# Graph attention with exponentials left unscaled: node products multiplied by inverse sums that TensorE spreads, and two kinds of splitting moved to GpSimd

## The reference

```python
h = (x @ W.T).reshape(n, heads, out_ch)
e = jax.nn.leaky_relu(a_src[src] + a_dst[dst], NEG_SLOPE)
m = jax.ops.segment_max(e, dst, num_segments=n)
ex = jnp.exp(e - m[dst])
denom = jax.ops.segment_sum(ex, dst, num_segments=n)
alpha = ex / (denom[dst] + EPS)
out = jax.ops.segment_sum(alpha[:, :, None] * h[src], dst, num_segments=n)
```

## Time and profile before

| | us |
|---|---|
| median of 3 executions | 1968.64 |
| lowest and highest | 1968.46, 1969.21 |
| profiled execution: span, first to last instruction | 1967.6 |
| loop of the first part in it, first peak to last score of tile 4 | 754 to 970 |
| busy in the whole span: PE, DVE, ACT, POOL | 1855.2, 1295.7, 934.8, 151.5 |

### The profile page before, as it was taken

How to read it: one execution, slowest core, us unless ns; L and a number is a source line. 1 busy time by engine, 2 the same in 40 slices (tenths; PEclk the granted TensorE clock), 3 DMA queues, 4 the chain that set the end, 5 groups by cost and what they waited for, 6 DMA issues and landing times.

```text
span 1967.6 us, 30950 instructions
## 1 busy us (share of the span) xinstructions
PE 1855.2 (94%) x12197; PEld 1758.9 (89%) x12198; DVE 1295.7 (66%) x2485; ACT 934.8 (48%) x1551; POOL 151.5 (8%) x127
## 2 busy tenths in 40 slices
PE   6987999999999999788799999999999999999998
PEld 5876789998889999787699999999999999999998
DVE  7997767555345656888865744456566667676886
ACT  2331222325134536878534232345555556666776
POOL 0000000004000023323100000000101001001010
PEclk9997999999999999899799999999999999999999
DMA  3110002101112112010131132154656566676795
GB/s 117 49 49 1 25 25 105 33 25 60 62 49 89 73 39 94 23 38 17 65 123 61 63 104 73 73 207 183 220 193 221 214 217 240 219 261 245 283 328 199
DMA packets 36844, 234.30 MB, mean 119 GB/s; under 512 B 5964, under 2 KB 7366, under 8 KB 14680
## 3 DMA queue, kind: packets, MB, share of 16 engines
q1 hardware_dynamic: 31366, 217.41, 30.8%
q0 software_dynamic: 2656, 8.99, 2.0%
q10 hardware_dynamic: 2674, 5.87, 0.8%
HBM read 221.91 MB, written 10.35 MB: 118 GB/s over the span
## 4 chain that ended last, share of the span: by engine, by line
PE 43%; issue 3%; DVE 3%; DMA 1%; ACT 1%; POOL 0%; ACTq 0%; POOLq 0%; DVEq 0%
PE bank L2734 8%; PE bank L341 7%; PE bank L342 7%; PE bank L343 7%; PE bank L2735 4%; PE bank L2746 3%; PE bank L2750 2%; PE bank L2738 2%; PE bank L2747 2%; PE bank L2749 1%; PE bank L2737 1%; DVE weight_lo L314 1%; PE bank L2692 0%; DMA out<-ffn_y,slot_token 0%; DMA weight_raw_fifth<-in_ffn_w 0%
## 5 line engine op out<-in xcount | busy, mean ns | idle before, releaser
L314 DVE TENSOR_TENSOR weight_lo<-weight_raw,weight_hi 128x2304 fp32r<-128x2304 f32 (+1 forms) x155 | 392.3, 2534 | 53.5 <-ACT weight_hi L304 53.2
L304 ACT ACTIVATE weight_hi<-weight_raw 128x2304 fp32r<-128x2304 f32 (+1 forms) x155 | 323.3, 2087 | 69.1 <-DMA weight_raw<-in_ffn_w 48.3
L341 PE MATMUL bank<-xT_hi,weight_hi 128*128 128x320 f32 (+1 forms) x576 | 182.8, 317 | 1.6 <-DVE xT_lo L362 1.4
L342 PE MATMUL bank<-xT_lo,weight_hi 128*128 128x320 f32 (+1 forms) x576 | 178.0, 309 | 0.0
L343 PE MATMUL bank<-xT_hi,weight_lo 128*128 128x320 f32 (+1 forms) x576 | 177.7, 309 | 0.0
L341 PE MATMUL bank<-weight_hi,xT_hi 128*128 128x384 f32 (+1 forms) x480 | 161.4, 336 | 11.2 <-DVE weight_lo L314 6.2
L3114 DVE TENSOR_TENSOR hidden_tmp<-hidden_tmp,bank 128x160 f32<-128x160 f32 (+5 forms) x192 | 65.6, 342 | 159.5 <-ACT hidden_tmp L2897 159.5
L342 PE MATMUL bank<-weight_lo,xT_hi 128*128 128x384 f32 (+1 forms) x480 | 157.3, 328 | 0.0
L343 PE MATMUL bank<-weight_hi,xT_lo 128*128 128x384 f32 (+1 forms) x480 | 157.0, 327 | 0.0
L615 PE MATMUL bank<-one_hot_dst,one_hot_src 125*128 125x313 f16 x800 | 123.5, 306 | 15.2 <-ACT packed_counts L629 7.9
L2897 ACT ACTIVATE hidden_tmp<-bank,ffn_b_by_load 128x160 f32<-128x160 f32 (+5 forms) x192 | 73.6, 404 | 119.8 <-PE bank L2738 114.2
(11 more groups left out here) (496 smaller groups left out, 5062.4 us busy)
## 6 DMA issues: line engine op xcount, KB each, us to landing
weight_raw<-in_ffn_w SPq DMA_DIRECT2D x111, 1152.0 KB, 5.1
weight_raw_fifth<-in_ffn_w SPq DMA_DIRECT2D x25, 1152.0 KB, 5.1
weight_raw<-in_shared_w SPq DMA_DIRECT2D x16, 1152.0 KB, 5.0
weight_raw<-in_mix_kv SPq DMA_DIRECT2D x8, 1152.0 KB, 5.0
weight_raw<-in_gat_w SPq DMA_DIRECT2D x8, 768.0 KB, 4.2
weight_raw<-in_mix_q SPq DMA_DIRECT2D x4, 1152.0 KB, 5.0
weight_raw<-in_mix_out SPq DMA_DIRECT2D x4, 1152.0 KB
weight_raw<-in_gnn_w SPq DMA_DIRECT2D x4, 1152.0 KB, 5.1
```

Source lines behind the costliest of these rows:

```text
L304: act.activation(upper_, whole_, ACT.Copy).then_inc(*w_hi.one())
L314: dve.tensor_tensor(lower_, whole_, upper_.bitcast(F32), ALU.subtract).then_inc(*w_lo.one())
L341: pe.matmul(dst, a[0], b[0], start=first, stop=False)
L342: pe.matmul(dst, a[0], b[1], start=False, stop=False)
```

## The change

Softmax weights are no longer formed. The exponentials go to TensorE as they are, two ticks earlier (lags 3, 4 and 5 for the transposes, the halves and the node product), and the product of a pair is multiplied afterwards by the inverse sums. These stand one to a destination node, and in the product the nodes are columns; so TensorE turns the column of sums, read 128 times over, against the identity into a bank, where each row then holds all 128 inverses (lag 4), ScalarE copies it to `inverse` (lag 5), and VectorE multiplies the node product from its bank by it (lag 6). ScalarE then rectifies from on-chip memory. VectorE adds 1e-16 (or 5e37 for a node without edges) and inverts, once for each pair. `ZS` falls from 7 buffers to 5, `LAST_LAG` from 10 to 8, the rectified values get a third slot, and the last `Y_AT` ticks of groups 2 and 3 are two earlier. The lower halves of the rectified values and the six chunks of `SPLIT` are subtracted by GpSimd, in the same loop as its terms. Renamed semaphores and lists are left out of the diff.

```diff
+def weight_lo_beside(i):
+whole_, upper_, lower_ = buffers(i)
+pool.wait_ge(w_hi.semaphore, i + 1)
+pool.wait_ge(w_lo.semaphore, i)
+pool.tensor_tensor(lower_, whole_, upper_.bitcast(F32), ALU.subtract).then_inc(*w_lo.one())
...
-ZS, XS = 7, DEPTH
+ZS, XS = 5, DEPTH
...
-zT = pair("gat_zT", [P, 2, 2, 2 * P], gat)
+zT = pair("gat_zT", [P, 3, 2, 2 * P], gat)
...
+inverse = count_f32[:, 2 * TP:2 * TP + 2 * P]
...
-LAST_LAG = 10
+LAST_LAG = 8
...
-Y_AT = {10 * grp + tick: (grp, t) for grp in range(4) for t, tick in enumerate((12, 13, 18, 19, 21) if grp < 3 else (12, 13, 16, 17, 18))}
+Y_AT = {10 * grp + tick: (grp, t) for grp in range(4) for t, tick in enumerate({2: (12, 13, 16, 17, 18), 3: (10, 11, 14, 15, 16)}.get(grp, (12, 13, 18, 19, 21)))}
...
+    return pairs_of[q][2] // 2
...
-    return (3 * grp + t0 // 2) % 2
-def sums_after(q):
-    grp, h, t0, n = pairs_of[q]
-    return y_full.at(2 * (grp * TT + t0 + n))
+    return y_full.at(2 * ((grp - 1) * TT + t0 + n))
...
-    for u in range(N1):
-        terms(u, *units[u][0:3])
+    for i in range(N1 + LAST_LAG):
+        if i < N1:
+            terms(i, *units[i][0:3])
+        if i in SPLIT:
+            weight_lo_beside(SPLIT[i])
+        q = pair_closing(i, 6)
+        if q is not None:
+            grp, h, t0, n = pairs_of[q]
+            hi, lo = at(zT, ALL, z_slot(q), h, slice(0, n * P))
+            pool.wait_ge(*z_hi.at(q + 1))
+            pool.tensor_tensor(lo, zt[:, q % 2, 0:n * P], hi.bitcast(F32), ALU.subtract).then_inc(*z_lo.one())
...
-        q = pair_closing(i, 7)
+        q = pair_closing(i, 5)
...
-            bank = ring.next(z_relu.at(q + 1))
+            bank = ring.next(z_scaled.at(q + 1))
...
-        u = unit(i, 5)
+        u = unit(i, 3)
         if u is not None:
-            turn_unit(u, e_scaled.at(u + 1))
+            turn_unit(u, e_exp.at(u + 1))
+        q = pair_closing(i, 4)
+        if q is not None:
+            grp, h, t0, n = pairs_of[q]
+            pe.wait_ge(*e_summed.at(q + 1))
+            bank = ring.next(inverse_kept.at(q + 1))
+            inverse_banks.append(bank)
+            for t in range(n):
+                end = pe.transpose(bank[:, t * P:(t + 1) * P], total[:, grp % 2, h, t0 + t:t0 + t + 1].broadcast_to([P, P]), ident[:, :])
+            end.then_inc(*inverse_full.one())
...
+        if grp > 1 and t == 0:
+            act.wait_ge(*aggregated(grp - 2))
...
-        q = pair_closing(i, 8)
-        if q is not None:
-            grp, h, t0, n = pairs_of[q]
-            act.wait_ge(*z_full.at(q + 1))
-            if q >= 2:
-                act.wait_ge(*z_lo.at(q - 1))
-            act.activation(zt[:, q % 2, 0:n * P], z_banks[q][:, 0:n * P], ACT.Relu, bias=b1[:, 2 * grp + h:2 * grp + h + 1]).then_inc(*z_relu.one())
-            act.wait_ge(*z_relu.now())
-            if q >= 4:
-                act.wait_ge(*sums_after(q - 4))
-            upper(at(zT, ALL, z_slot(q), h, slice(0, n * P)), zt[:, q % 2, 0:n * P]).then_inc(*z_hi.one())
...
-        u = unit(i, 6)
+        u = unit(i, 4)
         if u is not None:
             if u >= XS:
                 act.wait_ge(*z_full.at(units[u - XS][4] + 1))
             turned_upper(u, at(exT, ALL, u % XS, ALL, ALL))
-        u = unit(i, 4)
-        if u is not None:
-            grp, h, t = units[u][0:3]
-            e = edge_w[:, u % ZS, :]
-            act.wait_ge(*e_summed.at(u + 1))
-            act.activation(e, e, ACT.Copy, scale=total[:, grp % 2, h, t:t + 1]).then_inc(*e_scaled.one())
+        q = pair_closing(i, 5)
+        if q is not None:
+            n = pairs_of[q][3]
+            act.wait_ge(*inverse_full.at(q + 1))
+            if q:
+                act.wait_ge(*z_scaled.at(q))
+            act.activation(inverse[:, 0:n * P], inverse_banks[q][:, 0:n * P], ACT.Copy).then_inc(*inverse_kept.one())
+        q = pair_closing(i, 6)
+        if q is not None:
+            grp, h, t0, n = pairs_of[q]
+            act.wait_ge(*z_scaled.at(q + 1))
+            z = zt[:, q % 2, 0:n * P]
+            act.activation(z, z, ACT.Relu, bias=b1[:, 2 * grp + h:2 * grp + h + 1]).then_inc(*z_relu.one())
+            act.wait_ge(*z_relu.now())
+            if grp:
+                act.wait_ge(*sums_before(q))
+            upper(at(zT, ALL, z_slot(q), h, slice(0, n * P)), z).then_inc(*z_hi.one())
...
+        own_step(dve.tensor_scalar(least_sum[:, :], edge_peak[:, :], -1.0, 5.0e37, ALU.is_lt, ALU.mult))
+        own_step(dve.tensor_scalar(least_sum[:, :], least_sum[:, :], 1e-16, None, ALU.add))
...
-        q = pair_closing(i, 8)
+        q = pair_closing(i, 6)
         if q is not None:
...
-            dve.wait_ge(*z_hi.at(q + 1))
-            lower(at(zT, ALL, z_slot(q), h, slice(0, n * P)), zt[:, q % 2, 0:n * P]).then_inc(*z_lo.one())
-        u = unit(i, 6)
+            dve.wait_ge(*z_full.at(q + 1))
+            dve.wait_ge(*inverse_kept.at(q + 1))
+            if q >= 2:
+                dve.wait_ge(*z_lo.at(q - 1))
+            dve.tensor_tensor(zt[:, q % 2, 0:n * P], z_banks[q][:, 0:n * P], inverse[:, 0:n * P], ALU.mult).then_inc(*z_scaled.one())
+        u = unit(i, 4)
         if u is not None:
             turned_lower(u, at(exT, ALL, u % XS, ALL, ALL))
-        u = unit(i, 3)
-        if u is not None:
-            grp, h, t = units[u][0:3]
-            tot = total[:, grp % 2, h, t:t + 1]
-            dve.wait_ge(*e_exp.at(u + 1))
-            own_step(dve.tensor_scalar(tot, tot, 1e-16, None, ALU.add))
-            own_step(dve.reciprocal(tot, tot))
-            dve.tensor_tensor(tot, tot, has_edge[:, t:t + 1], ALU.mult).then_inc(*e_summed.one())
         u = unit(i, 1)
         if u is not None:
             peak(u, *units[u][0:3])
+        if pair_closing(i, 3) is not None:
+            grp, h, t0, n = pairs_of[pair_closing(i, 3)]
+            sums = total[:, grp % 2, h, t0:t0 + n]
+            dve.wait_ge(*e_exp.at(i - 3 + 1))
+            own_step(dve.tensor_tensor(sums, sums, least_sum[:, t0:t0 + n], ALU.add))
+            dve.reciprocal(sums, sums).then_inc(*e_summed.one())
...
-            weight_lo(SPLIT[i])
+            done["lo"] += 1
...
+            dve.wait_ge(w_lo.semaphore, c0 + 8)
```

More of the change, by code:

```diff
@@ L524, in counting_attention @@
          q_full, sums_ready, acted, q_ready, q_hi, q_lo, o_full, o_hi, o_lo, out_full, out_added, pads_blank, pads_hi, pads_lo) = sigs(
-            "one_hot_made", "one_hot_used", "counts_read", "edges_counted", "kv_full", "kv_copied", "kv_ready", "kv_hi", "kv_lo", "heads_full", "heads_kept",
+            "one_hot_made", "one_hot_used", "counts_read", "edges_counted", "kv_full", "kv_copied_or_inverse_full", "kv_ready", "kv_hi", "kv_lo", "heads_full", "heads_or_inverse_kept",
             "att_hi", "att_lo", "q_full", "q_low", "q_exp", "q_ready", "q_hi", "q_lo", "attended_full", "attended_hi", "attended_lo", "sum_full", "sum_added",
@@ L1831, in graph_attention @@
                  "att_rows_landed", "node_full", "node_hi", "node_lo", "scored", "score_turned", "score_hi", "score_lo", "rows_full", "rows_kept",
-                 "edge_acted", "edge_made", "edge_exp", "edge_summed", "edge_scaled", "ex_turned", "ex_hi", "ex_lo", "hidden_full", "hidden_acted", "hidden_hi", "hidden_lo",
+                 "edge_acted", "edge_made", "edge_exp", "edge_summed", "hidden_scaled", "kv_copied_or_inverse_full", "heads_or_inverse_kept", "ex_turned", "ex_hi", "ex_lo", "hidden_full", "hidden_acted", "hidden_hi", "hidden_lo",
                  "gat_y_full", "gat_y_added", "scored2", "h2_hi", "h2_lo", "gat_sum_full", "gat_sum_added")
@@ L1838, in graph_attention @@
          att_in, h_full, h_hi, h_lo, scored, score_turned, score_hi, score_lo, rows_full, rows_kept,
-         e_acted, e_made, e_exp, e_summed, e_scaled, ex_turned, ex_hi, ex_lo, z_full, z_relu, z_hi, z_lo,
+         e_acted, e_made, e_exp, e_summed, z_scaled, inverse_full, inverse_kept, ex_turned, ex_hi, ex_lo, z_full, z_relu, z_hi, z_lo,
          y_full, y_added, scored2, h2_hi, h2_lo, o_full, o_added) = sigs(*names)
@@ L1851, in graph_attention @@
         has_edge = sb("gat_has_edge", [P, TT], F32, gat)
+        least_sum = sb("gat_least_sum", [P, TT], F32, gat)
         scores = sb("gat_scores", [P, 2, TT, 4], F32, gat)
@@ L1892, in graph_attention @@
         h_banks, turn_banks, row_banks, ex_banks, z_banks, y_banks, o_banks = [], [], [], [], [], [], []
+        inverse_banks = []
         units, pairs_of = [], []
@@ L1944, in z_slot, with sums_before @@
         def z_slot(q):
+            return pairs_of[q][2] // 2
+        def sums_before(q):
             grp, h, t0, n = pairs_of[q]
-            return (3 * grp + t0 // 2) % 2
-        def sums_after(q):
-            grp, h, t0, n = pairs_of[q]
-            return y_full.at(2 * (grp * TT + t0 + n))
+            return y_full.at(2 * ((grp - 1) * TT + t0 + n))
         def w1_chunk(grp):
```

## The result

The changed kernel takes 1985.66 us (median of 4 executions, 1982.65 to 1987.15); the kernel before, beside it on the same chip, 1968.93 (1968.46 to 1972.5). The ratio is 1.0075, 95% interval 1.0054 to 1.0096: slower, where 1955.1 was forecast, and outside the range.

A forecast was written before the change was run, and what follows sets the result against it. ScalarE was taken to bound group 3, TensorE at a reduced clock ticks 15 to 19 and 25 to 29, no engine ticks 10 to 14 and 20 to 24. Terms -3 + 2 - 7.5 - 4 - 1 = -13.5 gave median 1955.1, range 1949 to 1963.

The forecast's parts named there:

- transposes come two ticks earlier: -1: Fill, 43.3 us with TensorE busy 38.93 on the stage before: earlier transposes save 1 us, bounds 0 and -3.
- a bank comes back a tick later as before: Ring of eight banks, one more bank per pair: costs nothing, at worst inside the bounds.
- Ticks 15 to 19 and 25 to 29: Stretches preparing the next group: 24.1 us each, 7.5 us less in all, bounds -12.4 and -2.
- the sum from five starts: TensorE's work in ticks 15 to 19 and 25 to 29, priced from five traced starts: 22.1 us at full clock.
- gain not there: Rival: TensorE's ticks stay but for moved products (-2), group 3 gains half; -3.5 us, median 1965; chance 13%.
- Ticks 10 to 14 and 20 to 24: Stretches where GpSimd takes over five weight chunks: 2 us more for both, bounds -3 and +8.
- Group 3: Up to its last peak, 35.90 us: ScalarE needs 5.2 less, of which 3 us is gained, bounds 0 and -5.2.
- Drain: After the last peak, 32.0 us: two ticks fewer save 4 us of idle, bounds 0 and -5.
- The shared read decides: Rival: GpSimd never lets VectorE in between instructions, each chunk costing the peak 5.3 us; +5.5, median 1974; chance 9%.
- The multiplication, which reads a bank: On VectorE: not held up by GpSimd, costs 0.44 us and replaces a lower half of 0.59.
- the 3.76 taken in proportion: GpSimd's price for a 1536-column weight chunk: 3.76 us, scaled from 1.567 for 640 columns, an upper end.
- the 0.63 in proportion: GpSimd's price for a pair's lower half of 256 columns: 0.63 us, scaled from its 640-column term.

The follow-up runs named there:

- e5: Changed kernel with VectorE's multiplication by the inverses moved ahead of the same tick's preparations; 1975.26 us, ratio 1.0027 to the kernel before.
- e2: Changed kernel with the old lags (transposes 5, halves 6, product 7, multiplication 8); 1973.88 us, ratio 1.0025 to the kernel before.
- e6: Changed kernel with the old lags and the multiplication ahead of the same tick's preparations; 1964.95 us, ratio 0.9963 to the kernel before.
- e7: As e6, with the weight chunks' lower halves back on VectorE; 1960.93 us, ratio 0.9949 to the kernel before.
- e10: As e5 (short lags, early multiplication), with the weight chunks' lower halves back on VectorE; 1971.69 us, ratio 1.0005 to the kernel before.
- e1: Changed kernel with the halves of units 0 and 1 made at the end of tick 5; 1983.57 us, ratio 1.0067 to the kernel before.
- e11: As e10, with the halves of units 0 and 1 made at the end of tick 5; 1965.38 us, ratio 0.9984 to the kernel before.
- e9: As e7, with the pairs' lower halves back on VectorE too, so no splitting on GpSimd; 1963.37 us, ratio 0.9964 to the kernel before.
- e8: Changed kernel with the old lags and all lower halves back on VectorE, leaving the scaling alone; 1976.10 us, ratio 1.0023 to the kernel before.
- e3: Changed kernel with both kinds of splitting (weight chunks and pairs' lower halves) back on VectorE; 1990.02 us, ratio 1.0102 to the kernel before.
- e4: Kernel before, with only the weight chunks and the pairs' lower halves moved to GpSimd; 1974.60 us, ratio 1.0013 to the kernel before.

## Why the prediction was wrong

**The lags in the fill: forecast -1, measured +13.0, most of the miss.** The step that failed is "transposes come two ticks earlier: -1". The program order moved, TensorE did not: it is busy with the projections until 773 to 774 in either kernel. What moved was ScalarE's dependence on it, from its tick 6 to its tick 4, and the first node product, to ahead of the first prepared tile. With lag 6 ScalarE and VectorE ran through units 0 to 3 beside the projections (the peak of unit 3 started at 764.99 in the kernel before, at 776.29 after). The first prepared tile then starts 30.3 us behind the first peak, where it was 22.0: 8.3 of the 13.0, and most of the rest is the bank (e5 takes 4.5 from the fill). I had the 38.93 of 43.30 busy as a floor and not as a queue that others now wait for. That the lags are the cause is shown by e2 (fill 43.3) and, with the other cause removed, by e6 against e5 and e7 against e10 (-10.3 and -10.8 us). The part of unit 0's halves alone is 2 us of the 8.3 (e1, e11).

**The bank: forecast "nothing", measured about 9 to 13 us** (e5 under the changed kernel 10.4, e6 under e2 8.9, e9 under e8 12.7; 9.5, 12.2 and 11.6 by the ratios). The step was "a bank comes back a tick later as before". It did come back in the same tick, but I counted ticks and not places in a queue: it was ScalarE's to give, ahead of VectorE by 1.9 us, and is now VectorE's, behind its preparations; and one more bank a pair brings the ring round sooner (this second part is argued from the order, no run took it alone). This is the wait that took the place of the one removed.

**Ticks 15 to 19 and 25 to 29: forecast -7.5, measured +5.5.** The working, 22.1 us of TensorE at full clock and 2 for pauses, took for granted that nothing new stops TensorE. With the bank free (e6) the two are 27.3 and 29.3 against 27.8 and 28.8 before: level. So the gain forecast there does not exist either. In e6 they run at clock 1.00 with PE busy near 25 us, not 22.1: the sum from five starts was too low by about 3 us a stretch, and the other 2.5 to 4.3 us are idle in turns between the three engines. One term is plainly wrong. The sum has two node products where it counts three before, and a saving from that; the traces have three in either kernel, before two of 256 columns and one of 128, after all three of 256 (45 matmuls, 15 on each line of `mm3`), so there was nothing to save and 1.8 us was left out. The spread source rows were left out too. Nor did the pause in front go with VectorE's chunk: TensorE still waits 2.4 us for VectorE's lower halves at the start of both stretches, where it had been up to 3.2. So no gain was to be had there, and that much of the rival "gain not there", given 13%, was true.

**Ticks 10 to 14 and 20 to 24: forecast +2, measured +1.2.** Right in sum; TensorE's wait for GpSimd's chunk, 4.97 us where it had been 2.03 for VectorE's, was no term of it.

**Group 3: forecast -3, measured -0.5.** The gain exists: with the old lags the stretch takes 31.5 to 32.4 (e2, e6 to e9), with the short ones 32.3 where the bank is free and the chunks are VectorE's (e10, e11). With the short lags and either of these as changed it stays at 35.4 to 35.6 (e1, e3, e5). In the changed kernel the first four intervals between its peaks take 3.8, 4.6, 4.7 and 4.4 us and the later six about 3.0. The excess is TensorE at half its clock. VectorE's stretched peak, TensorE's first matmul behind its wait, and the windows view of the time after it:

```profile
917.69 2.79 DVE L2359 CUSTOM_DVE_ANT_0 gat_edge<-gat_edge,edge_terms 128x640 f32<-128x640 f32 x1
922.50 0.38 PE L361 MATMUL bank<-gat_rowT_hi,row_selector 2*128 2x320 f32 x1 [2.41 <-DVE gat_rowT_lo L369]
923.30:930.00 6.70, 6.70 (x26) 6.27 (x25) 5.13 (x13) 5.20 (x12) 5.16 (x4) 0.50 0.37 108
```

The chunk of tick 28 holds the peak for 2 us; VectorE's halves of the source rows stand behind that peak, TensorE waits 2.41 us for them and then works 6.7 us at a granted clock of 0.50. In e5 it is the same (a pause of 2.6 us, clock 0.51 from 911.3 to 918), though its ticks 25 to 29 take only 29.5. In e10, with the chunk on VectorE, the pause is 0.44 us and the seven us behind it run at 1.00:

```profile
911.00:918.00 7.00, 7.00 (x49) 6.77 (x48) 5.62 (x14) 6.82 (x17) 5.43 (x4) 1.00 0.25 69
```

The step missed is that the chunk of tick 28 was charged to a peak, and not to the next group's source rows and the clock behind them. It is not the whole of it: e2 has the same pause of 2.41 us and takes 32.4, and e3 is slow here without a GpSimd chunk, behind two pauses of 1.5 and 1.1 us. Why the half clock lasts under 4 us in e2 stays open. ScalarE at 83% is no longer the bound, as forecast.

**Drain: forecast -4, measured -4.4.** Right, as a sum: the short lags give 3.3 of it (e2), and what they take from the drain TensorE has to do in the fill.

**The rival that got the sign had the wrong mechanism.** "The shared read decides" assumed that GpSimd goes from one instruction to the next without letting VectorE in. The timelines of GpSimd and VectorE after, at the first chunk:

```profile
815.98 3.43 POOL L321 TENSOR_TENSOR weight_lo<-weight_raw,weight_hi 128x1536 fp32r<-128x1536 f32 x1 [0.75 <-ACT weight_hi L304]
...
817.12 2.98 DVE L2359 CUSTOM_DVE_ANT_0 gat_edge<-gat_edge,edge_terms 128x640 f32<-128x640 f32 x1
...
819.38 2.14 POOL L2007 TENSOR_TENSOR edge_terms<-gat_edge_log,gat_src_row 128x640 f32<-128x640 f32 x1
```

The peak asks at 817.12, waits for the chunk to end at 819.41, then runs, and it is the GpSimd term behind it that is stretched, to 2.14 from 1.57. The peak loses 2.98 - 0.83 = 2.15 us to a chunk, not 5.3. That rival's 1974 was 12 us short as well, and outside the 1941 to 1971 that I gave with the rivals at both ends. The multiplication, which reads a bank, kept 0.42, as forecast.

## What to carry to other kernels

When a reader of a buffer changes engine, write down what stands ahead of the reader in the new engine's queue, within the tick; a wait that was "a tick later as before" can be 2 to 3 us later, and in a ring the engine that pays is the one that comes round. Shortening lags takes away lead: before costing it at nothing, find the stretch where the feeding engine is busy with something else and ask who will now stand and wait for it. And test a change of several parts by taking each back alone: here a scaling worth 7 us (e9 against the kernel before), hidden by one line's place and by the lags, looked like a loss of 17. And a cost read at one wait is not settled by it: the long wait of the changed kernel was nearly as long before.

## What was not expected of the hardware

A subtraction of 128x1536 took GpSimd 3.43 to 3.53 us in five cases and 4.08 in one (mean 3.46 in e4), under the 3.76 taken in proportion from its 128x640. The Trainium skill ("GPSIMD Engine Reference", Performance versus the Vector engine), from which 3.37 was estimated, lies nearer to five of the six. For the small instruction it is the other way: a pair's 128x256 lower half took 0.94 us on average (0.73 in e4), over the 0.63 in proportion.

A VectorE instruction of one column with both operands in on-chip memory can take as long as GpSimd's instruction beside it: the sum of a pair of one took 965 ns on average (L2431, 128x1, eight of them, the longest 3.45 beside a chunk), where the former column took 226. It now stands right behind the peak, as here after the one shown above:

```profile
820.02 1.51 DVE L2431 TENSOR_TENSOR gat_total<-gat_total,gat_least_sum 128x1 f32<-128x1 f32 x1
```

It ends with GpSimd's term (819.38 + 2.14 = 821.52).
